# Sixteen-head cross-attention of a gated transformer block: one score pass with exponentials kept by row, or two score passes with transposed exponentials

## The chip, the cores and the metric

The kernel runs on one core of one Trainium2 chip. The metric is the device time of one execution in microseconds (us); several runs are taken and their median is the number compared.

## The reference, cut to what matters

Two layers act on x of 4 batches x 512 tokens x 128 features, with a context of 4 x 77 rows. The second layer's attention is what the change touches; 16 heads of 8 features attend to the 77 context rows of the batch:

```python
Q = split(LN(x) @ W_q.T); K = split(ctx @ W_k.T); V = split(ctx @ W_v.T)   # 16 heads, 8 wide
scores = einsum('bhqd,bhkd->bhqk', Q, K) / sqrt(8)
scores = where(mask, -inf, scores)          # mask (1, 1, 512, 77)
w = nan_to_num(softmax(scores, -1), nan=0)
x = x + tanh(g_xattn[1]) * (merge(einsum('bhqk,bhkd->bhqd', w, V)) @ W_o.T)
x = x + tanh(g_ffn[1]) * moe(LN(x))          # router (24 columns per token), best 2 of 8 experts, silu(a)*g
```

Ahead of it stand a first layer's single-head attention and a quantised feed-forward layer; behind it 39 expert tiles of 128 rows.

## The kernel before, in words

The program is one hand-ordered list per engine: TensorE (`pe`), VectorE (`dve`), ScalarE (`act`), GpSimd (`pool`) and SyncE (`sp`, loads and stores), tied by semaphores. An engine takes its list strictly in order, so a wait holds back all that stands behind it. PSUM has eight banks of 512 f32: `bank[0]` to `bank[3]` and the four of `wide`.

**Keys and values.** The 16 heads are four groups of four. Group g has its 32 features on partitions 32g to 32g+31 (`qT`, `kblk`), and its 4 x 77 = 308 score columns. `kblk` holds the keys block-diagonally within a group; `vblk` does so for the values, cut into `NCH` = 12 chunks of 103 or 102 score columns (three to a group).

**Attention of a batch, before.** `scores(b, u)` on TensorE (L649, L652) makes a unit of 128 queries x two groups: two bf16 matmuls lay the mask into two banks of `wide`, and two f32 matmuls, each on 32 rows of the array, add the scores. A batch has `UNITS` = 8 units in two buffers. `softmax(b, u)` on VectorE takes the head maxima (L1015) and writes score minus maximum to `pC` in SBUF (L1018); `expC` on ScalarE (L450) makes the exponentials in place; `sums` (L1024) adds them by head, and `sums_end` takes the reciprocals. Then `turn_p(b, c)` on TensorE (L673) turns each of the 12 chunks in four transposes into `bank[2]` or `bank[3]`, `copy_pT` on ScalarE (L458) copies it to SBUF, and `pv(b, t)` (L688) multiplies four chunks at once, in four strips of 32 output rows, into `bank[1]`. The reciprocals are turned and spread over the features by `turn_r`, `copy_rT`, `spread_r`, `copy_rE`; `attn_out` (L1040) multiplies. `wo` (L717) projects, `residual` (L1044) adds to x and takes the statistics and the reciprocal root of the next norm on VectorE.

**Router of a batch.** Step 0 normalises (L867), transposes (L725) and copies; step 1 multiplies by the router weights (L730) and picks experts in a chain of small VectorE operations (L1057 to L1087); step 2 ranks them (L738, L739) and makes the slots (L1091 to L1106). Then `send(b)` on GpSimd writes the batch's rows out with 8 indirect DMAs (L370). `router(b, 0)` waits, from batch 2 on, for the rows of batch b-2.

**Order.** A period n = 0..11 of batch b issues `turn_p(b, n)`, then, for the first eight, unit n of batch b+1, then `pv`. The wo, residual and router steps of batch b-1 stand at fixed slots of the period of batch b (`WO_SLOT`, `NORM_SLOT`, `ROUTER_SLOTS`). Ahead of the first period, the four queries are made (L537, L663) while GpSimd supplies the reciprocal roots (`rsqrt`, L349 to L355) and VectorE finishes the feed-forward layer. Behind the last period stand `wo(3)`, `residual(3)`, the three router steps of batch 3 and `send(3)`; only when all rows have landed do the expert tiles start.

## Time and profile before

| what | us |
|---|---|
| median of 3 runs | 430.97 |
| the three runs | 431.97, 430.97, 419.12 |
| the profiled execution | 425.74 |
| its span, from the first instruction to the last | 424.0 |
| TensorE busy in it | 284.7 |
| VectorE busy in it | 260.5 |
| ScalarE busy in it | 124.3 |
| GpSimd busy in it | 94.5 |
| mean granted TensorE clock, share of full speed | 0.727 |

All rows come from the profiled execution. Its own time is 1.7 us more than its span, and the median of the runs is 5.2 us more than its time. PE is TensorE's matmul, PEld its weight load, DVE VectorE, ACT ScalarE, POOL GpSimd, SP SyncE. A f32 matmul shows as two records (two passes), a bf16 matmul and a transpose as one.

### The profile page before, as it was taken

What the parts mean: (1) busy time and instruction counts of PE and PEld (TensorE: products, weight loads), DVE (VectorE), ACT (ScalarE), POOL (GpSimd) and SP (SyncE); (2) the same over time, 40 slices, a digit from 0 to 9 for tenths busy, and PEclk for the clock granted to TensorE, in tenths of its full rate; (3) what the DMA queues carried; (4) which work ended last, traced back from release to release, by engine and by line L of the source; (5) the groups of instructions that cost most, each with busy time, mean ns of one, the idle gap of its engine ahead of it and who ended that gap; (6) DMA issues with size and microseconds to landing.
All of it is one profiled execution on the core that took longest, in us unless ns stands there. A gap on an engine that the chain in (4) does not pass through costs nothing.

```text
span 424.0 us, 5379 instructions
## 1 busy us (share of the span) xinstructions
PE 284.7 (67%) x1571; PEld 197.0 (46%) x1572; DVE 260.5 (61%) x754; ACT 124.3 (29%) x240; POOL 94.5 (22%) x157
## 2 busy tenths in 40 slices
PE   1158824634689798989798875732039998999920
PEld 0158712113233343545355434412038998989920
DVE  5746995987737887597769854755403433444424
ACT  1022105435215354423343243301023333333300
POOL 8300000003710000000250033060602444434420
PEclk9999965556555598755675567565559999999975
DMA  7993001500000000000010000010356767768337
GB/s 225 364 336 115 2 5 8 138 1 0 1 2 0 0 2 0 2 0 0 12 41 0 0 22 32 0 51 0 100 175 195 210 204 199 210 198 226 109 97 206
DMA packets 34787, 36.96 MB, mean 87 GB/s; under 512 B 8990, under 2 KB 26901, under 8 KB 34767
## 3 DMA queue, kind: packets, MB, share of 16 engines
q1 hardware_dynamic: 30607, 23.73, 20.7%
q0 software_dynamic: 4160, 12.99, 8.7%
q8 instruction: 9, 0.15, 0.1%
q14 instruction: 11, 0.09, 0.1%
HBM read 22.52 MB, written 14.49 MB: 87 GB/s over the span
## 4 chain that ended last, share of the span: by engine, by line
PE 43%; DVE 35%; issue 8%; DMA 5%; POOL 4%; ACT 3%; SPq 1%; POOLq 0%; DVEq 0%; ACTq 0%
PE wide L786 13%; PE bank L795 6%; PE bank L673 4%; PE wide L652 4%; DVE space L1018 3%; DVE mC L1015 3%; PE bank L688 3%; DVE st L838 2%; DVE amh L989 2%; DVE h L867 2%; DVE space L985 2%; DVE sC L1024 2%; DMA space<-expert_out 2%; PE bank L717 2%; POOL expert_rows L370 2%
## 5 line engine op out<-in xcount | busy, mean ns | idle before, releaser
L370 POOL DMA_INDIRECT expert_rows<-pay,slot x32 | 30.8, 963 | 158.9 <-DVE slot L1106 150.4
L1156 DVE TENSOR_TENSOR space<-space,wide 128x384 f32<-128x384 f32 x39 | 21.6, 554 | 66.0 <-PE wide L786 55.2
L786 PE MATMUL wide<-space,w1r 128*128 128x128 f32 x468 | 60.8, 281 | 0.0
L786 PEld LDWEIGHTS wide<-space,w1r 128*128 128x128 f32 x468 | 57.0, 197 | 0.4
L379 POOL DMA_INDIRECT expert_out<-space x39 | 38.3, 982 | 60.9 <-DVE space L1163 60.6
L673 PE MATMUL bank<-ident,space 128*103 128x128 f32 (+1 forms) x192 | 42.0, 368 | 13.2 <-ACT pTC L458 7.1
L673 PEld LDWEIGHTS bank<-ident,space 128*103 128x103 f32 (+1 forms) x192 | 32.0, 211 | 33.5 <-issue 16.3
L450 ACT ACTIVATE space<-space 128x616 f32<-128x616 f32 x32 | 22.8, 716 | 58.5 <-DVE space L1018 58.3
L652 PE MATMUL wide<-kblk,h2T 32*128 32x308 f32 x128 | 38.1, 686 | 0.0
L1015 DVE TENSOR_REDUCE mC<-wide 128x8 f32<-128x616 f32 x32 | 25.4, 795 | 19.3 <-PE wide L652 16.4
L458 ACT ACTIVATE pTC<-bank 103x512 f32<-103x512 f32 (+1 forms) x48 | 27.8, 587 | 23.6 <-PE bank L673 16.2
L795 PE MATMUL bank<-w_s,space 128*128 x234 | 32.6, 275 | 0.2 <-DVE space L1156 0.2
L537 PE MATMUL bank<-ident,h 128*128 128x128 f32 x48 | 13.3, 433 | 28.6 <-DVE h L867 27.8
L795 PEld LDWEIGHTS bank<-w_s,space 128*128 128x128 f32 x234 | 29.3, 192 | 0.3 <-issue 0.3
L505 ACT ACTIVATE space<-bank 128x128 f32<-128x128 f32 x39 | 10.8, 277 | 60.7 <-PE bank L771 58.3
L1018 DVE TENSOR_TENSOR space<-wide,mC 128x616 f32<-128x616 f32 x32 | 25.6, 799 | 1.1
L771 PE MATMUL bank<-ident,space 128*128 128x128 f32 x39 | 11.4, 293 | 21.7 <-DMA space<-expert_rows 17.2
L537 PEld LDWEIGHTS bank<-ident,h 128*128 128x128 f32 x48 | 8.6, 217 | 35.8 <-DVE h L867 34.9
L511 ACT ACTIVATE space<-wide 128x384 f32<-128x384 f32 x39 | 19.1, 490 | 17.0 <-PE wide L786 16.2
L1024 DVE TENSOR_REDUCE sC<-space 128x16 f32<-128x1232 f32 x16 | 22.5, 1425 | 0.0
L649 PE MATMUL wide<-mneg,identb 128*128 128x308 bf16 x64 | 19.8, 404 | 1.5 <-DVE space L1018 1.5
L349 POOL TENSOR_SCALAR rvp<-mv 128x4 f32<-128x4 f32 x4 | 0.9, 224 | 87.0 <-DVE mv L841 86.6
(205 smaller groups left out, 432.9 us busy)
## 6 DMA issues: line engine op xcount, KB each, us to landing
w1r<-in_w1T SPq DMA_DIRECT2D x39, 352.0 KB
expert_rows<-blank POOLq DMA_DIRECT2D x2, 2970.0 KB, 18.3
expert_rows<-blank POOLq DMA_DIRECT2D x1, 2574.0 KB, 28.3
space<-expert_rows SPq DMA_DIRECT2D x39, 66.0 KB
space<-expert_out SPq DMA_DIRECT2D x8, 256.0 KB, 3.2
xs<-in_x SPq DMA_DIRECT2D x4, 256.0 KB, 3.8
w_s<-in_w2T SPq DMA_DIRECT2D x2, 512.0 KB, 5.1
out<-xs SPq DMA_DIRECT2D x4, 256.0 KB, 3.4
```

The source lines that it names most:

```text
L370: pool.indirect_dma_start(tbl, bass.IndirectOffsetOnAxis(ap=slot[:, k, t:t + 1], axis=0), pay[:, b % 2, k, j, :], None).then_inc(rows_sent ...
L379: pool.indirect_dma_start(planes, bass.IndirectOffsetOnAxis(ap=mpay[:, j, D:D + 1].bitcast(I32), axis=0), my[:, j, :], None, bounds_check= ...
L450: act.activation(p, p, ACT.Exp, scale=float(DH) ** -0.5).then_inc(pC_ready, 1)
L458: act.activation(pTC[0:w, q % (2 * NG), :], bank[2 + q % 2][0:w, :], ACT.Copy).then_inc(pTC_ready, 1)
L537: ins = pe.transpose(bank[0][:, j * P:(j + 1) * P], src[:, j, :], ident[:])
L652: ins = pe.matmul(o[i], qT[r, b, j * P:(j + 1) * P], kblk[r, :, b * KS:(b + 1) * KS], start=False, stop=True)
L673: ins = pe.transpose(bank[2 + q % 2][0:w, j * P:(j + 1) * P], pC[:, (b * TB + j) % (2 * TB), c0:c0 + w], ident[:])
L786: ins = pe.matmul(wide[:, 2 * p + g, c * P:(c + 1) * P], w1r[:, q, g * F + F0[c]:g * F + F0[c] + P], mhT[:, p, :])
L795: ins = pe.matmul(bank[1 + p][:, 0:D], mhidT[:, p, c, :], w2_s[:, bass.ds(w + c * D, D)], start=(c == 0), stop=(c == NF - 1))
L1015: link(dve.tensor_reduce(m.rearrange("p (g l) -> p g l", g=2), s, AX.X, ALU.max))
L1018: dve.tensor_tensor(pC[:, t % (2 * TB), (u % 2) * HU:(u % 2 + 1) * HU].rearrange("p (g l k) -> p g l k", g=2, l=HG), s, m.rearrange("p (g ...
L1024: dve.tensor_reduce(sC[:, j, :], pC[:, (b * TB + j) % (2 * TB), :].rearrange("p (h k) -> p h k", h=H), AX.X, ALU.add).then_inc(sums_done, 1)
```

## The change

**Two score passes.** The first pass only finds maxima: `quad_max(b, j)` makes the scores of 128 queries and all four groups, four mask matmuls and then four f32 matmuls on the four 32-row strips of the array, and `max_of` takes the maxima in two reductions. `split_max` clips them at FLOOR, negates them and splits them into three bf16 parts that stand in `comb` beside the mask; `turn_max` transposes `comb` (bf16), `copy_comb` copies it. The second pass, `quad_exp(b, t)`, makes the scores transposed, keys on partitions and 512 queries in the free dimension: four bf16 matmuls of `pick` with `combT` lay down minus maximum and mask, four f32 strip matmuls add the scores. `expT` takes the exponential straight from PSUM to `pT`, four of 103 (or 102) x 512. There are no transposes of p, no subtraction, no `expC` over SBUF and no copies of p.

**Sums.** `pv` works in two halves of 256 queries; beside the four matmuls with `vblk` it has four with `hones`, which leave each head's sum beside the output in the same bank. `recip` on ScalarE takes Ln (with a bias TINY) and Exp(-x), and `attn_out` on VectorE corrects it by one step, three operations of 128 x 256 for each half. `turn_r`, `spread_r` and their copies go.

**Banks.** The quads take two pairs of banks each from a ring of three pairs (`wide` and the new `duo`). Quad n waits until the second pair of quad n-2 and the first pair of quad n-1 are read.

**Order.** The four quads of maxima of batch 0 are made among the queries. A period of batch b is: exp 0, pv half 0 of b-1, max 0 and 1 of b+1, pv half 1 of b-1, rank of b-2, exp 1, max 2, wo of b-1, max 3, exp 2, turn_max(b+1), router steps 0 and 1 of b-1. So a router begins at the end of a period and ends in the next one; behind the last period stand the second half of router 2's step 1, its step 2, and all of router 3. `misc` keeps the users of `bank[0]` apart. The next norm's reciprocal roots of batches 0 and 1 move from VectorE to GpSimd, ahead of `send(0)` in its list. GpSimd also makes `hones` and `pick`, by memsets and six affine selects, and copies the mask. One activation table with both Ln and Exp is loaded by hand ahead of the first exponential.

```diff
-    UNITS = 2 * TB
-    RT_SLOT, WO_SLOT, NORM_SLOT, ROUTER_SLOTS = 0, 2, 4, (5, 6, 9)
+    NPART = 3
+    KM = NPART * H
+    KROWS = KM + KS
+    HS = S // 2
+    TR = NCH // NG
...
+        quads = [("max", 0, j) for j in range(TB)]
+        for b in range(NB):
+            for t in range(TR):
+                quads.append(("exp", b, t))
+                if b + 1 < NB and t < 2:
+                    quads += [("max", b + 1, 2 * t), ("max", b + 1, 2 * t + 1)]
+        pairs = [wide[:, 0:2, :], wide[:, 2:4, :], duo[:]]
...
-            for n in range(2 * NB, 3 * NB):
+            for n in range(2 * NB, 3 * NB + 2):
                 rsqrt(n)
...
+            def expT(b, t, pair_no):
+                if pair_no == 0:
+                    act.wait_ge(sT_psum, TR * b + t + 1)
...
+                for i in range(2):
+                    c = NG * t + 2 * pair_no + i
+                    w = HCH[c][1]
+                    act.activation(pT[0:w, (NCH * b + c) % (2 * NCH), :], pair("exp", b, t, pair_no)[0:w, i, :], ACT.Exp,
+                                   scale=float(DH) ** -0.5).then_inc(pT_ready, 1)
+            def recip(b, half):
...
+                act.activation(lnS[:, n % 2, :], obank(b, half)[:, HS:S], ACT.Ln, bias=tiny[:]).then_inc(ln_ready, 1)
+                act.wait_ge(ln_ready, n + 1)
+                act.activation(rE[:, n % 2, :], lnS[:, n % 2, :], ACT.Exp, scale=-1.0).then_inc(rE_ready, 1)
...
+            def pairs_free(n):
+                for place in (2 * n - 3, 2 * n - 2):
+                    if place >= 0:
+                        pe.wait_ge(*emptied(place))
+            def quad_max(b, j):
...
+                for g in range(NG):
+                    pe.matmul(o[g].rearrange("p (l k) -> p l k", l=HG), identb[:],
+                              mneg[:, j, None, :].broadcast_to([P, HG, KS]), start=True, stop=False)
+                for g in range(NG):
+                    r = slice(32 * g, 32 * g + 32)
+                    ins = pe.matmul(o[g], qT[r, b, j * P:(j + 1) * P], kblk[r, b, :], start=False, stop=True)
+                ins.then_inc(sC_psum, 1)
...
+            def quad_exp(b, t):
...
+                for g in range(NG):
+                    pe.matmul(o[g], pick[0:KROWS].rearrange("p h k -> p (h k)")[:, g * GC:(g + 1) * GC][:, keys(t)],
+                              combT[0:KROWS, b % 2, :], start=True, stop=False)
+                for g in range(NG):
+                    r = slice(32 * g, 32 * g + 32)
+                    ins = pe.matmul(o[g], kblk[r, b, keys(t)], qT[r, b, :], start=False, stop=True)
+                ins.then_inc(sT_psum, 1)
...
                 for g in range(NG):
-                    pe.matmul(bank[1][32 * g:32 * g + 32, :], vblk[0:w, c, b, :], pTC[0:w, (q + g) % (2 * NG), :],
-                              start=(t == 0), stop=(t == 2)).then_inc(pv_done, 1)
+                    pe.matmul(o[32 * g:32 * g + 32, 0:HS], vblk[0:w, NG * t + g, b, :], pT[0:w, (q + g) % (2 * NCH), cols],
+                              start=(t == 0), stop=False)
+                for g in range(NG):
+                    ins = pe.matmul(o[32 * g:32 * g + 32, HS:S], hones[0:w, t, :], pT[0:w, (q + g) % (2 * NCH), cols],
+                                    start=False, stop=(t == TR - 1))
...
+            for b in range(NB - 1):
+                quad_exp(b, 0)
+                if b >= 1:
+                    for t in range(TR):
+                        pv(b - 1, 0, t)
+                quad_max(b + 1, 0)
+                quad_max(b + 1, 1)
+                if b >= 1:
+                    for t in range(TR):
+                        pv(b - 1, 1, t)
+                if b >= 2:
+                    router(b - 2, 2)
+                quad_exp(b, 1)
+                quad_max(b + 1, 2)
+                if b >= 1:
+                    wo(b - 1)
+                quad_max(b + 1, 3)
+                quad_exp(b, 2)
+                turn_max(b + 1)
+                if b >= 1:
+                    router(b - 1, 0)
+                    router(b - 1, 1)
...
+            def max_of(b, j):
+                dve.wait_ge(sC_psum, TB * b + j + 1)
+                for i in range(2):
+                    dve.tensor_reduce(mC[:, b % 2, j, i * 2 * HG:(i + 1) * 2 * HG].rearrange("p (g l) -> p g l", g=2),
+                                      pair("max", b, j, i)[:, :, 0:GC].rearrange("p g (l k) -> p g l k", l=HG),
+                                      AX.X, ALU.max).then_inc(max_ready, 1)
...
+            def split_max(b):
...
+                link(dve.tensor_scalar(c[:, :, 0:H], m, FLOOR, -1.0, ALU.max, ALU.mult))
+                link(dve.scalar_tensor_tensor(out=mR[:], in0=m, scalar=FLOOR, in1=c[:, :, 0:H], op0=ALU.max, op1=ALU.add))
+                link(dve.tensor_scalar(c[:, :, H:2 * H], mR[:], -1.0, None, ALU.mult))
+                dve.scalar_tensor_tensor(out=c[:, :, 2 * H:KM], in0=mR[:], scalar=-1.0, in1=c[:, :, H:2 * H],
+                                         op0=ALU.mult, op1=ALU.subtract).then_inc(split_ready, 1)
+            def attn_out(b, half):
...
+                link(dve.tensor_tensor(z, o[:, HS:S], r, ALU.mult))
+                link(dve.scalar_tensor_tensor(out=z, in0=z, scalar=-2.0, in1=r, op0=ALU.add, op1=ALU.mult))
+                dve.scalar_tensor_tensor(out=oT[:, half * HS:(half + 1) * HS], in0=o[:, 0:HS], scalar=-1.0, in1=z,
+                                         op0=ALU.mult, op1=ALU.mult).then_inc(oT_ready, 1)
...
+            b = NB - 1
+            router(b - 2, 1, 0)
+            attn_out(b - 1, 0)
+            router(b - 2, 1, 1)
+            attn_out(b - 1, 1)
+            router(b - 2, 2)
+            residual(b - 1)
+            router(b - 1, 0)
+            router(b - 1, 1, 0)
+            attn_out(b, 0)
+            attn_out(b, 1)
+            residual(b)
+            router(b - 1, 1, 1)
+            router(b, 0)
+            router(b - 1, 2)
+            for step in range(1, 3):
+                router(b, step)
```

## Rows read from the trace of the kernel before

**Rows 1.** The page: granted clock in tenths, 40 slices of 10.6 us.
```profile
PEclk9999965556555598755675567565559999999975
```

**Rows 2.** Groups by form: busy us, mean ns | idle us before, releaser.
```profile
L370 POOL DMA_INDIRECT expert_rows<-pay,slot x32 | 30.8, 963 | 158.9 <-DVE slot L1106 150.4 <-issue 8.5
...
L673 PE MATMUL bank<-ident,space 128*103 128x128 f32 x128 | 27.5, 353 | 6.0 <-issue 3.2 <-ACT space L450 2.7
L1018 DVE TENSOR_TENSOR space<-wide,mC 128x616 f32<-128x616 f32 x32 | 25.6, 799 | 1.1
L1015 DVE TENSOR_REDUCE mC<-wide 128x8 f32<-128x616 f32 x32 | 25.4, 795 | 19.3 <-PE wide L652 16.4 <-issue 2.8
...
L1024 DVE TENSOR_REDUCE sC<-space 128x16 f32<-128x1232 f32 x16 | 22.5, 1425 | 0.0
...
L458 ACT ACTIVATE pTC<-bank 103x512 f32<-103x512 f32 x32 | 18.6, 585 | 16.8 <-PE bank L673 9.4 <-remote 4.1 <-PE bank L688 3.3
...
L479 ACT ACTIVATE qk<-qk 128x256 f32<-128x256 f32 x4 | 1.7, 416 | 8.1 <-DVE qk L1062 8.1
...
L349 POOL TENSOR_SCALAR rvp<-mv 128x4 f32<-128x4 f32 x4 | 0.9, 224 | 87.0 <-DVE mv L841 86.6 <-POOL rstd L355 0.3
```

**Rows 3.** Windows: us, busy (x records) of PE, PEld, DVE, ACT, POOL; PEclk; DMA.
```profile
119.00:142.00 23.00, 19.27 (x55) 6.48 (x53) 16.25 (x23) 8.35 (x12) 0.00 (x0) 0.50 0.00 0
...
184.00:204.70 20.70, 16.28 (x64) 9.07 (x62) 18.31 (x50) 7.47 (x14) 0.00 (x0) 0.50 0.00 0
204.70:225.00 20.30, 19.29 (x88) 10.49 (x88) 13.54 (x44) 6.99 (x13) 7.86 (x8) 0.67 0.08 27
312.60:405.00 92.40, 86.41 (x736) 84.67 (x737) 34.87 (x77) 31.20 (x79) 36.35 (x37) 0.97 0.66 188
```

**Rows 4.** Timeline of PE, attention: start us, us, line, operands, records, idle.
```profile
125.21 2.07 PE L663 MATMUL bank<-hT,wqT_s 128*128 128x512 f32 x2 [0.69 <-ACT hT L391]
...
131.01 0.69 PE L649 MATMUL wide<-mneg,identb 128*128 128x308 bf16 x2
131.63 1.40 PE L652 MATMUL wide<-kblk,h2T 32*128 32x308 f32 x4
132.96 0.69 PE L649 MATMUL wide<-mneg,identb 128*128 128x308 bf16 x2
...
142.40 1.18 PE L673 MATMUL bank<-ident,space 128*103 128x128 f32 x4 [2.73 <-ACT space L450]
...
160.16 1.07 PE L688 MATMUL bank<-pTC,vblk 103*32 103x512 f32 x8
...
169.06 0.68 PE L673 MATMUL bank<-ident,space 128*103 128x128 f32 x4
...
171.54 0.43 PE L649 MATMUL wide<-mneg,identb 128*128 128x308 bf16 x2
171.90 0.79 PE L652 MATMUL wide<-kblk,h2T 32*128 32x308 f32 x4
...
206.58 3.31 PE L688 MATMUL bank<-pTC,vblk 103*32 103x512 f32 x16
209.82 0.68 PE L673 MATMUL bank<-ident,space 128*103 128x128 f32 x4
...
238.54 1.94 PE L688 MATMUL bank<-pTC,vblk 103*32 103x512 f32 x8
...
250.75 0.68 PE L673 MATMUL bank<-ident,space 128*103 128x128 f32 x4
```

**Rows 5.** Timeline of DVE: router 2, then behind the last pv of batch 3.
```profile
267.84 0.42 DVE L1065 TENSOR_REDUCE qks<-qk 128x32 f32<-128x256 f32 x1 [0.48 <-ACT qk L479]
...
272.51 0.17 DVE L1087 CAST ohs<-qkm 128x32 bf16<-128x32 f32 x1
...
278.23 0.69 DVE L1040 TENSOR_TENSOR oT<-bank,rE 128x512 f32<-128x512 f32 x1 [3.70 <-PE bank L688]
...
298.13 0.17 DVE L1106 CAST slot<-slotf 128x8 int32<-128x8 f32 x1
```

More of the change, by code:

```diff
@@ L210, in flamingo_kernel, with pair, emptied, obank @@
         tbl_v = tbl.rearrange("(p n r) c -> p n (r c)", p=P, r=3)
+        quads = [("max", 0, j) for j in range(TB)]
[4 more added lines that the diff above has]
+                    quads += [("max", b + 1, 2 * t), ("max", b + 1, 2 * t + 1)]
+        quad_no = {q: n for n, q in enumerate(quads)}
+        pairs = [wide[:, 0:2, :], wide[:, 2:4, :], duo[:]]
+        def pair(kind, b, k, i):
+            return pairs[(2 * quad_no[kind, b, k] + i) % 3]
+        def emptied(place):
+            kind, b, k = quads[place // 2]
+            if kind == "max":
+                return max_ready, 2 * (TB * b + k) + place % 2 + 1
+            return pT_ready, NG * (TR * b + k) + 2 * (place % 2 + 1)
+        def obank(b, half):
+            return bank[2] if b == NB - 1 and half else bank[1][:]
+        def keys(t):
+            return slice(THIRD * t, THIRD * t + HCH[NG * t][1])
         def xb(b):
@@ L318, in _ @@
                                     pattern=[[1, P]], channel_multiplier=-1))
-            for t, p_, c_, n_ in ((headof, 1, -DH, H), (spread, -DH, 1, P)):
+            for t, p_, c_, n_ in ((headof, 1, -DH, H),):
                 link(pool.memset(t[:], 1.0))
@@ L677, in pv @@
-            def pv(b, t):
+            def pairs_free(n):
[3 more added lines that the diff above has]
+            def quad_max(b, j):
+                n = quad_no["max", b, j]
+                if n == 0:
+                    pe.wait_ge(mneg_ready, 1)
+                if n == 1:
+                    pe.wait_ge(dn_ready, NB)
+                if j == 0:
+                    pe.wait_ge(q_ready, b + 1)
+                pairs_free(n)
+                o = [pair("max", b, j, g // 2)[:, g % 2, 0:GC] for g in range(NG)]
+                for g in range(NG):
[5 more added lines that the diff above has]
+                ins.then_inc(sC_psum, 1)
@@ new lines, in turn_max @@
+            def turn_max(b):
+                misc(combT_ready, b + 1)
+                pe.wait_ge(split_ready, b + 1)
+                if b == 0:
+                    pe.wait_ge(mneg_copied, 2)
+                for j in range(TB):
+                    ins = pe.transpose(bank[0][:].bitcast(BF16)[0:KROWS, j * P:(j + 1) * P], comb[:, b % 2, j, :], identb[:])
+                ins.then_inc(comb_psum, 1)
+            def quad_exp(b, t):
+                if b == 0 and t == 0:
+                    pe.wait_ge(pick_made, 1)
+                if t == 0:
+                    pe.wait_ge(combT_ready, b + 1)
+                pairs_free(quad_no["exp", b, t])
+                w = HCH[NG * t][1]
+                o = [pair("exp", b, t, g // 2)[0:w, g % 2, :] for g in range(NG)]
+                for g in range(NG):
[5 more added lines that the diff above has]
+                ins.then_inc(sT_psum, 1)
@@ new lines, in _ @@
+            b = NB - 1
+            quad_exp(b, 0)
+            for t in range(TR):
+                pv(b - 1, 0, t)
+            quad_exp(b, 1)
+            for t in range(TR):
+                pv(b - 1, 1, t)
+            router(b - 2, 2)
+            quad_exp(b, 2)
+            wo(b - 1)
+            for t in range(TR - 1):
+                for half in range(2):
+                    pv(b, half, t)
+            router(b - 1, 0)
+            router(b - 1, 1)
+            for half in range(2):
+                pv(b, half, TR - 1)
@@ L1047, in residual, with router @@
                 stats(3 * NB + b)
-            def router(b, step):
+            def router(b, step, half=None):
                 pb = pay[:, b % 2]
@@ L1054, in router @@
                     normalise(3 * NB + b, pb[:, 0, :, 0:D])
-                if step == 1:
+                if step == 1 and half != 1:
                     dve.wait_ge(mix_psum, b + 1)
@@ L1063, in router @@
                                       ALU.subtract).then_inc(qkm_ready, 1)
+                if step == 1 and half != 0:
                     dve.wait_ge(qke_ready, b + 1)
```

330 lines of the change are left out of this document (147 added, 183 removed).

## The prediction

> **What bounds the kernel now.** I read four views in turn. The page's clock slices show TensorE's clock at full speed over the expert tiles and near half over most of the attention, slices 12 to 29 [rows 1]. The windows then show why attention is the place to look: a period of a middle batch takes 40.8 and 40.9 us, from the first transposes at 169.06 to those at 209.82 and 250.75 [rows 4], and two windows that make up such a period (184.0 to 225.0) have TensorE busy 35.6 us (16.28 + 19.29) and VectorE 31.9 us (18.31 + 13.54) at clocks of 0.50 and 0.67, against 0.97 over the expert tiles [rows 3]. So TensorE is nearly full, but at half speed, and VectorE is close behind. The groups say what VectorE does there: maxima, subtractions and sums are 25.4, 25.6 and 22.5 us, and TensorE has 192 transposes of p, 128 of them 27.5 us [rows 2]. The timeline prices the pieces at both speeds. ScalarE and GpSimd have room. The change acts from the first query to the last send; what lies before and behind stays.
>
> **TensorE, work by work.** I give each price at the low clock and, after a slash, at the high one.
>
> A pair of mask matmuls takes 0.62 / 0.36 us (131.01 to 131.63; 171.54 to 171.90), a pair of f32 score matmuls on two strips 1.33 / 0.72 (131.63 to 132.96; 0.79 less the 0.07 by which 1.40 exceeds 1.33) [rows 4]. The trace has no four-strip matmul. Below, it costs what the pair does, since the two of the pair run side by side (four records, 1.40 us); above, twice that. I take the lower end, because pv runs four strips side by side already: 8 records of 512 columns in 1.94 us at the low clock, 1.07 at the high [rows 4]. A quad of maxima is then 2 x 0.62 + 1.33 = 2.6 / 1.4, where the two units it replaces take 3.9 / 2.2. A quad of exponentials has 512 columns for 308: four pick matmuls 1.9 / 1.1, four strips 2.1 / 1.1 (both scaled by columns, less what a pair loses at its ends), together 4.0 / 2.2.
>
> What a page would change in this stands here alone: the Trainium skill, TensorE: Matmul & The Clock Gate, section Measured speedup vs the span model, has four K=32 row tiles of 512 columns gain 3.07 times and not four. By it and the query's matmul (two records in 2.07 us, about 1.87 between starts), a strip set is 4 / 3.07 x 1.87 = 2.4 us and not 2.1, and the sum is about 3 us higher. No row here shows four.
>
> pv of a batch has 3 x 4 matmuls of 512 columns now, about 1.74 / 0.87 a set (the times above less 0.2 of lag); afterwards twice the columns, so 10.4 / 5.2 instead of 5.2 / 2.6. The four bf16 transposes of maxima are an estimate of 0.6 / 0.4. Gone are 12 x 4 transposes of p, about 0.98 / 0.48 each set (1.18 and 0.68 less 0.2) [rows 4], and an estimated 2 us of turned and spread reciprocals. Per middle batch: 4 x 2.6 + 3 x 4.0 + 10.4 + 0.6 = 33.4 against 8 x 1.95 + 11.8 + 5.2 + 2 = 34.6 low; 17.8 against 18.5 high. With wo and router, an estimate of 5.2 / 2.6 on both sides, it is 38.6 / 20.4. **TensorE's work is not cut.** The time can come only from its waits and its clock.
>
> **VectorE and ScalarE.** VectorE loses eight subtractions of 0.80, four sums of 1.43 [rows 2], 0.8 of reciprocals and attn_out's 0.69 [rows 5]: 13.6 us of 31.9. It gains split_max (four small operations, 0.9) and attn_out in six operations of 256 columns at 0.42 plus links (0.42 from L1065 [rows 5]), 2.8: about 22 us. ScalarE has twelve exponentials of 512 columns in place of twelve copies (0.585 each [rows 2]) and eight exponentials; recip is four of 256 columns (at most 0.42 each, L479). It stays under 15 us a batch. One table load stands where one stood.
>
> **The ring.** A quad needs the first pair of the quad just before it read: 0.795 for a reduction, about 1.1 for two exponentials, unless other work lies between. That is a new wait at TensorE, and everything in its list is queued behind it. In batch 0's period nothing lies between: seven waits, 7 us. In a middle period pv or wo cover about half: 4 us. VectorE serves in order too, so a quad of maxima can also wait for router or attn_out chains; 1 to 2 us.
>
> **The clock.** From 119 to 142 us TensorE is busy 19.3 of 23 us, mostly on two-strip scores, at 0.50; the expert tiles, full array, get 0.97 [rows 3]. In the middle batches it was low up to a pv of 16 records at 206.58, and the transposes at 209.82 take 0.68 against 1.18 at 142.40 [rows 4]. [...] The new quads use all four strips, the mask and pick matmuls all rows, pv doubles. I take the high clock for half of each middle period. Both ends (none, all) are rivals below.
>
> **The sum**, against the profiled execution's 425.7 us:
> - Start. The quads of batch 0 fill the waits between queries, TensorE's work is 4 x 2.6 instead of 8 x 1.95, and VectorE's last subtractions, sums and exponentials no longer stand ahead of the first transposes at 142.40. In place come two reductions, split_max, transposes and a copy (about 3.5 us). Bounds 131 and 138; I take 135: -7.4.
> - Period of batch 0, low clock: 3 x 4.0 + 4 x 2.6 + 7 = 29.3 for 26.7 (142.40 to 169.06): +2.6.
> - Two middle periods. Half the time at each clock, 38.6 / 20.4 takes 1 / (0.5/38.6 + 0.5/20.4) = 26.7; with 5.3 of waits 32.0 for 40.85: -17.7.
> - Period of batch 3, 27.5 now (250.75 to 278.23). No maxima of a next batch, but pv of two batches: 3 x 4.0 + 20.8 + 5.2 = 38 / 19.6, at half and half 26, waits 4: +2.5.
> - Tail, 20.1 now (278.23 to 298.30) [rows 5]. attn_out is 2.1 longer. Because routers begin at a period's end, the second half of router 2's step 1 now stands there as well: L1065 at 267.84 to L1087 at 272.68, 4.8 us. Waits for bank 0 and router 2's last step beside router 3's matmuls, 1.4. +8.3.
> - send(2), eight DMAs of 0.96 + 0.30 = 10.1 us [rows 2], starts some 11 us before slot 3 is ready, so it is just hidden; without that, 10.1 us more at most.
> - GpSimd's constants stand in front of an idle time of 86.6 us [rows 2]: nothing. Its two extra reciprocal roots make the next norm later by an estimated 2 us each, at a period's end, inside the waits above; send(0) queues behind them and has a period of slack.
>
> Sum -7.4 + 2.6 - 17.7 + 2.5 + 8.3 = -11.7, so 414.0 us. The runs shown have a median 5.2 above the profiled time and a lowest 6.6 below; I leave the sum where it is and keep that spread for the range.
>
> **Rivals.**
>
> *A, the clock goes up and stays.* For: the argument above, doubled; against: ring waits open gaps. Then the start gives -9, batch 0's period 3 x 2.2 + 4 x 1.4 + 7 = 19.2 (-7.5), the middle ones are bound by VectorE's 22 us and the order of its list, about 30 (-21.7), batch 3 28 (+0.5), tail +8.3: -29.4, 396 us. [...]
>
> *B, slower: the clock stays low through attention.* Place: the three later periods. Middle ones 38.6 + 3 = 41.6 (+0.8 each), batch 3's 38 with the waits mostly hidden against 27.5 (+9.5 to 10.5), start -6, batch 0 +2.6, tail +8.3: about +16, 442 us. It decides from a high share of about a quarter downwards. For: 119 to 142 us at 0.50 with TensorE 84% busy; against: the pv that raised it.
>
> *C, the strips run two by two.* A set costs twice: 16 x 1.0 + 12 x 1.6 at mean clock, 35 us, of which some 5 hide in ring waits: 414 + 30 = 444 us. Against: pv.
>
> *D, waits eat the gain.* If the ring and VectorE's order cost 6 us more in each middle period, it is 426 us. A rule of the skill leans this way: TensorEngine Tiling (Array Packing), Key Properties, says a change of tiling mode drains TensorE; each quad has two. In the trace that drain is inside the 0.62 and 1.33.
>
> **How the numbers follow.** Forecast 0.38, A 0.24, B 0.14, C 0.06, D 0.18. A measurement of this kernel can tell about 2% from no change. The forecast is 2.7% faster and falls within 2% in one case of six; D lies within, with small parts to either side. Faster 0.57, same 0.21, slower 0.22. The range reaches to A and to B: 395 to 440 us; the forecast's own is 405 to 422.
>
> **What would show it.** Right: in a middle period about 32 us with TensorE's clock near 0.75; four-strip sets (eight records) near 1.4 us at the low clock for 308 columns; VectorE busy about 22 us a period and no subtraction group; seven waits near 1 us before quads in batch 0's period; 28 us from the last batch's first attn_out to slot 3. Wrong: four-strip sets of 2.7 us (C), a clock of 0.50 throughout (B) or 1.0 throughout (A), GpSimd still in send(2) when slot 3 is ready.

## The result, and the profile after

The changed kernel takes 419.69 us (median of 20 runs, 417.02 to 421.40), the kernel before 427.77 us (median of 20, 418.65 to 431.97). The ratio is 0.9928, 95% interval 0.9901 to 0.9955: 0.7% faster, no difference at 2%. It is not the quotient of the two medians (0.981), because it leaves out slow runs, those well above the fastest of the same kernel, and only the kernel before had any: it compares with some 422.7 us (419.69 / 0.9928). The forecast was 414.0 us, 2.7% less than the profiled 425.7. The profiled execution took 420.08 us, span 418.3 (before 425.74 and 424.0).

The page's slices, in tenths. The first line is TensorE's row before, the others are the changed kernel's; the clock row answers to [rows 1]. TensorE is busy less in the middle of the span (260.0 us in all, 284.7 before) and clocked higher (0.781 on average, 0.727 before):

```profile
PE   1158824634689798989798875732039998999920
```

```profile
PE   0158725655486668867877974411059899989910
PEclk9999975556568568896887997555559999999975
```

Windows of the changed kernel, one for each step of the forecast: batch 0's period, the two middle ones, batch 3's, and the tail from batch 3's first attn_out to the start of the last send. Columns as in [rows 3]:

```profile
133.50:162.20 28.70, 20.73 (x88) 7.03 (x89) 6.87 (x12) 5.74 (x12) 0.00 (x0) 0.60 0.00 1
162.20:192.70 30.50, 22.63 (x204) 11.35 (x205) 12.26 (x31) 10.47 (x21) 2.77 (x14) 0.91 0.00 1
192.70:227.40 34.70, 26.76 (x208) 13.15 (x208) 19.70 (x75) 9.95 (x21) 5.90 (x17) 0.80 0.01 5
227.40:263.40 36.00, 27.41 (x251) 12.97 (x251) 16.50 (x79) 10.66 (x23) 12.67 (x14) 0.83 0.08 27
263.40:292.80 29.40, 6.01 (x33) 4.58 (x25) 21.26 (x117) 2.83 (x7) 7.67 (x9) 0.50 0.06 19
```

| step | forecast | measured | missed by |
|---|---|---|---|
| first exp quad | 135 us | 133.5 us | -1.5 |
| period of batch 0 | 29.3 | 28.7 | -0.6 |
| two middle periods | 64.0 | 65.2 | +1.2 |
| period of batch 3 | 30.0 | 36.0 | **+6.0** |
| tail | 28.4 | 29.4 | +1.0 |

Four of five steps lie within 1.5 us. Batch 3's period holds nearly the whole error (6.0 us; the four others add up to 0.1). TensorE's timeline in that period shows it: pv sets of eight records come every 0.43 us, and from 249.28 us on, matmuls come one or two at a time, behind gaps for which the profile has no releaser ("issue"):

```profile
248.41 0.61 PE L796 MATMUL bank<-space,hones 103*32 103x256 f32 x8
248.85 0.61 PE L793 MATMUL duo<-space,vblk 103*32 103x256 f32 x8
249.28 0.76 PE L796 MATMUL duo<-space,hones 103*32 103x256 f32 x2
250.36 0.59 PE L796 MATMUL duo<-space,hones 103*32 103x256 f32 x2 [0.32 <-issue]
251.11 0.38 PE L796 MATMUL duo<-space,hones 103*32 103x256 f32 x1 [0.16 <-issue]
251.83 0.42 PE L796 MATMUL duo<-space,hones 103*32 103x256 f32 x2 [0.34 <-issue]
253.25 0.38 PE L796 MATMUL duo<-space,hones 103*32 103x256 f32 x1 [1.00 <-issue]
253.55 0.68 PE L813 MATMUL bank<-ident,pay 128*128 128x128 f32 x2
254.68 0.43 PE L813 MATMUL bank<-ident,pay 128*128 128x128 f32 x2 [0.45 <-issue]
258.49 1.87 PE L819 MATMUL bank<-wqkv_s,hT 128*128 128x24 f32 x8 [3.38 <-ACT hT L443]
```

The chain of waits goes through it as a piece without a name, 10.46 us ahead of ScalarE's copy of router 2's hT:

```profile
245.21 2.06 ACT space L513 x4
247.26 10.46 another core or an unknown queue
257.75 0.60 ACT hT L443
```

The last two transposes are recorded at 254.68, but the copy that waits for them starts 3 us later; ends of matmuls are modelled, so the true ends, or their signals, came later than the rows say. GpSimd's rows say what ran beside it. send(1), eight DMAs, stood from 246.15 to 256.0 us:

```profile
246.15 0.96 POOL L422 DMA_INDIRECT expert_rows<-pay,slot  x1 [12.25 <-DVE slot L1224]
...
255.02 0.96 POOL L422 DMA_INDIRECT expert_rows<-pay,slot  x1 [0.30 <-issue]
```

The trace of before has the same sign beside its own send(1), and it stood in the rows of the forecast: "issue 3.2" at L673 and "remote 4.1" at L458 [rows 2]. Nothing was made of it.

### The profile page after: what moved, and what is told of

Its sections match the earlier page's. It is cut to its first block, busy times and chain, and to the rows that moved or that the text cites. A ratio compares the mean times of both kernels' runs of the same rounds, so it can differ in the third digit from the quotient of the medians.

```text
span 418.3 us, 5818 instructions
## 1 busy us (share of the span) xinstructions
PE 260.0 (62%) x1803; PEld 177.2 (42%) x1804; DVE 219.4 (52%) x710; ACT 105.9 (25%) x220; POOL 107.9 (26%) x193
## 4 chain that ended last, share of the span: by engine, by line
PE 45%; DVE 29%; issue 8%; ACT 5%; POOL 5%; DMA 5%; another core or an unknown queue 3%; SPq 1%; POOLq 0%; DVEq 0%
PE wide L901 13%; POOL expert_rows L422 3%; PE duo L910 3%; PE bank L910 3%; DVE h L982 3%; DVE st L953 2%; DVE mC L1116 2%; ACT space L513 2%; PE wide L750 2%; PE wide L772 2%; DVE amh L1103 2%; DMA space<-expert_out 2%; DVE space L1099 2%; PE bank L793 2%
## 5 line engine op out<-in xcount | busy, mean ns | idle before, releaser
L1116 DVE TENSOR_REDUCE mC<-wide 128x8 f32<-128x616 f32 x22 | 16.9, 791 | 26.2 <-PE duo L750 17.5
L513 ACT ACTIVATE space<-wide 103x512 f32<-103x512 f32 (+1 forms) x32 | 17.0, 601 | 29.0 <-PE wide L776 18.4
L982 DVE TENSOR_SCALAR h<-xs,mv,rstd 128x128 f32<-128x128 f32 x48 | 17.1, 421 | 4.3 <-POOL rstd L391 4.1
L776 PE MATMUL wide<-h2T,kblk 32*103 32x512 f32 (+1 forms) x64 | 17.7, 802 | 0.0
L910 PE MATMUL bank<-w_s,space 128*128 x120 | 16.8, 276 | 0.2 <-DVE space L1287 0.2
L953 DVE BATCH_NORM_STATS2 st<-xs 128x6 f32<-128x128 f32 x64 | 13.8, 279 | 5.2 <-DMA xs<-in_x 4.8
L750 PE MATMUL wide<-kblk,h2T 32*128 32x308 f32 x88 | 16.5, 606 | 0.0
L746 PE MATMUL wide<-mneg,identb 128*128 128x308 bf16 x44 | 11.1, 368 | 8.6 <-DVE mC L1116 3.9
L513 ACT ACTIVATE space<-duo 103x512 f32<-103x512 f32 (+1 forms) x16 | 8.7, 601 | 28.4 <-PE wide L776 28.4
L793 PE MATMUL bank<-space,vblk 103*32 103x256 f32 (+1 forms) x168 | 15.6, 449 | 0.4 <-DVE oT L1156 0.4
## 6 DMA issues: line engine op xcount, KB each, us to landing
space<-expert_out SPq DMA_DIRECT2D x8, 256.0 KB, 3.3
xs<-in_x SPq DMA_DIRECT2D x4, 256.0 KB, 3.7
out<-xs SPq DMA_DIRECT2D x4, 256.0 KB, 3.4
```

The lines of the kernel that those rows point to most:

```text
L513: act.activation(pT[0:w, (NCH * b + c) % (2 * NCH), :], pair("exp", b, t, pair_no)[0:w, i, :], ACT.Exp, scale=float(DH) ** -0.5).then_inc( ...
L750: ins = pe.matmul(o[g], qT[r, b, j * P:(j + 1) * P], kblk[r, b, :], start=False, stop=True)
L793: pe.matmul(o[32 * g:32 * g + 32, 0:HS], vblk[0:w, NG * t + g, b, :], pT[0:w, (q + g) % (2 * NCH), cols], start=(t == 0), stop=False)
L910: ins = pe.matmul(bank[1 + p][:, 0:D], mhidT[:, p, c, :], w2_s[:, bass.ds(w + c * D, D)], start=(c == 0), stop=(c == NF - 1))
L953: ins = dve.bn_stats(st[:, n % 2, j, :], xs[:, (n % NB) * TB + j, :])
L982: ins = dve.tensor_scalar(dst[:, j, :], xs[:, (n % NB) * TB + j, :], mv[:, n, j, 0:1], rstd[:, n, j:j + 1], ALU.subtract, ALU.mult)
```

## The experiments

Kernels of one series ran one after the other on one chip, with the kernel before beside them. The first series is e1 to e4; the changed kernel itself was in none until e12, so up to there its 419.69 us is a number of another series. (The expectations say "call" for a series.)

**1. Is it the instruction fetch?** The trace lists 16 KB packets of TensorE's instruction queue at 232.3 and 247.5 us, each inside a send. 128 increments at the start of TensorE's list move them; 256 put them back.

```diff
+            for _ in range(128):
+                pe.sem_inc(pad, 1)
             pe.wait_ge(ident_made, 1)
             pe.wait_ge(ld_ctx, 48)
             pe.matmul(wide[:, 0, 0:NB * KS], wbT_s[:], ctxT_s[:]).then_inc(mA_psum, 1)
+            for _ in range(128):
+                pe.sem_inc(pad, 1)
```

e1 has the first loop, e2 both.

> The changed kernel with 128 semaphore increments (on a semaphore that nobody waits for) put ahead of TensorE's first wait, where TensorE stands idle until 9.5 us; all else is the same. They move TensorE's program on by 128 instructions, and with it the places at which the instruction queue (q8 in the list of DMA packets) fetches the next 16 KB: from 232.3 and 247.5 us, both beside a send, to about 218 and 240 us, beside none. Theory F (TensorE starves when a fetch falls beside a send of GpSimd): the stall of 249.3 to 257.7 us is gone, batch 3's period takes about 30 us for 36.0, and the time is 412 to 415 us for 419.7. Theory S (a send holds up TensorE or its semaphores whatever TensorE fetches): the stall stays, 419 to 421 us.

> The control of e1_pad128: 256 such increments, 128 ahead of the first matmul and 128 behind it, so that the fetches fall where they fell in the changed kernel. Theory F: the stall is back, 419 to 421 us. If added instructions at the start had an effect of their own (a different clock, a later first matmul), this run would differ from 419.7 us too; then e1_pad128 says less.

e1 422.39 us (10 runs), e2 439.00. The increments take 0.15 us each and were not free: TensorE's first matmul comes at 20.5 us for 9.6, the first exp quad at 135.5 and 153.1 us for 133.5. From there to the end all three take the same, 285.0, 284.2 and 284.8 us. In e1 the packets came at 228.7, 241.3 and 261.4 us, none in send(1) (248.2 to 258.0), and ScalarE still waited:

```profile
ACT hT L444 <- remote: 10.4, 1, 10.4
```

Theory F falls. (The unchanged kernel in e12, below, says it once more: packets at 232.0 and 247.3 us, beside the sends, and no stall.) The Trainium skill (Runtime: NRT & Kernel Launch, Instruction fetch mechanics) has instructions refilled in blocks of 16 KiB, at a cost mostly hidden; that agrees with these packets and with their place making no difference. A fault of the pair: e2 was meant as a costless control and cost 19 us.

**2. Is it the send?** One wait more on GpSimd:

```diff
             for b in range(NB):
+                if b == 1:
+                    pool.wait_ge(mix_read, 3)
                 send(b)
```

> The changed kernel with one more wait on GpSimd: send(1) also waits until router 2's mix is copied (about 255 us if the stall goes), so that nothing is sent beside TensorE's fetch at 247.5 us. Theory F and theory S both take the stall away: 412 to 416 us. Theory B (the boundary of 16 KB alone stalls TensorE, whatever GpSimd does) and theory W (a wait of the new order, not the chip, holds TensorE back): the stall stays, 419 us or more.

414.49 us (4 runs, 413.06 to 415.51). send(1) ran from 253.6 to 263.6 us, and the same stretch of TensorE is whole:

```profile
246.98 0.61 PE L798 MATMUL duo<-space,hones 103*32 103x256 f32 x8
249.59 0.73 PE L815 MATMUL bank<-ident,pay 128*128 128x128 f32 x4 [2.00 <-DVE pay L984]
251.10 1.87 PE L821 MATMUL bank<-wqkv_s,hT 128*128 128x24 f32 x8 [0.78 <-ACT hT L445]
```

Router 2's mix stands 27.9 us behind the first exp quad of its period, for 33.1. So it is the send beside TensorE's work, not the boundary of the fetch (B) and not a wait of the new order (W). How dense that work must be no run tests: the kernel before pauses beside its send(1) too, with sparser work.

**3. Why does VectorE start late?** In the changed kernel one operation on 128 x 16 values (`rv`) takes 4.29 us and ends when GpSimd's memset of `pay` does; the first eight normalises take 6.0 us for 2.3 while GpSimd makes `pick`. First VectorE, then GpSimd:

```profile
9.59 4.29 DVE L969 TENSOR_SCALAR rv<-mv 128x16 f32<-128x16 f32 x1
...
16.49 6.02 DVE L982 TENSOR_SCALAR h<-xs,mv,rstd 128x128 f32<-128x128 f32 x8
```

```profile
8.77 1.40 POOL L372 MEMSET vblk<- 128x1536 f32 x1
...
12.00 1.85 POOL L379 MEMSET pay<- 128x2112 f32 x1
...
16.18 4.46 POOL L405 TENSOR_SCALAR_AFFINE_SELECT pick<-pick 128x1232 bf16<-128x1232 bf16 x3
```

```diff
+            pool.wait_ge(h_ready, 2)
             pool.memset(vblk[:], 0.0).then_inc(vblk_zero, 1)
```

> The changed kernel with GpSimd's work from the memset of vblk to the last select of pick behind a wait for VectorE's first two normalised batches. Theory P (VectorE's tensor_scalar stands still, or goes slower, while GpSimd writes tensors): VectorE's rv takes 0.2 us for 4.3, the first eight normalises 2.3 us for 6.0, and all behind comes 6 to 8 us earlier: 412 to 414 us. Theory Q (the 4.3 us are VectorE's wait for something of its own, such as a load): rv still takes 4 us or more, 418 to 420 us.

413.86 us (4 runs), with the stall still in it. VectorE's rows, `rv` 25 times shorter and the normalises 2.7 times:

```profile
9.56 0.17 DVE L970 TENSOR_SCALAR rv<-mv 128x16 f32<-128x16 f32 x1
...
12.26 2.26 DVE L983 TENSOR_SCALAR h<-xs,mv,rstd 128x128 f32<-128x128 f32 x8
```

Eight microseconds are won there; 5.6 arrive at the first exp quad (127.8 us): batch 2's normalises still stand 7.3 us ahead of the changed kernel's, the weights' maxima 5.9. Theory P holds. The Trainium skill (SBUF — State Buffer, SBUF: two separate sides) has VectorE, in some of its operations, and GpSimd share a pair of ports under an exclusive lock, where the loser blocks for the whole instruction. The trace agrees that rv is blocked, but for more than one instruction: it began during the memset of `vblk` (8.77 to 10.17 us) and ended only with that of `pay`, the sixth GpSimd operation after it (13.88 us). Other operations are not slowed: the small tensor_tensors from 14.8 us on take 0.17 beside GpSimd's memset of `pick` (14.91 to 16.03), as in e4. That ports are what they share is the skill's account; the runs show the blocking alone.

The price of the constants that the change itself adds, alone:

```diff
+            pool.wait_ge(h_ready, 2)
             link(pool.memset(hones[:], 1.0))
```

> The changed kernel with only the constants that the change adds on GpSimd (the row-sum ones and pick) behind the wait for VectorE's first two normalised batches; the memsets that the kernel before has too stay where they were. If e4's gain of 5.8 us is two parts, this one is the smaller: VectorE's rv still takes 4.1 us (behind the old memsets), the first eight normalises 2.3 us for 6.0, and the attention comes about 2 to 3 us earlier: 416.5 to 418 us for 419.7. If the selects of pick hold VectorE up wherever they stand, the normalises of batches 2 and 3 take it instead and nothing is gained.

413.12 us: far more gained than expected, 6.6 us less than the changed kernel. The attention began 1.5 us earlier (132.0 for 133.5; one profile says little here, as three profiles of the unchanged kernel have 133.5, 133.3 and 131.3), and, unforeseen, the stall was gone. That had to be explained before anything else was read.

**4. A first answer that fell.** In the changed kernel, e1 and e4 TensorE had run some 115 to 120 records, matmuls and weight loads together, from send(1)'s start when it stalled. To see whether their number matters, the middle third of batch 3's keys was left out of pv:

```diff
-            for t in range(TR - 1):
-                for half in range(2):
-                    pv(b, half, t)
+            for half in range(2):
+                pv(b, half, 0)
```

> The changed kernel with the sixteen key-third-1 groups of batch 3's value product left out (both halves, products and sums alike), so that TensorE has some 64 records fewer between the start of send(1) and router 2's transposes; batch 3's attention then lacks those keys. In the four traces with a stall TensorE had run 115 to 119 records from the send's first instruction when it began to trickle. Theory C (what stalls TensorE is the number of its instructions beside a send): with about 80 records ahead of the transposes they run at once behind router 2's normalise (251.9 us), hT is copied by 254 us and router 2's mix by 256 us for 260.5. Theory D (any instruction of TensorE that falls a few microseconds into a send is held until the send ends): the transposes' semaphore comes about 1.7 us behind the send's end again, the mix at 260 us.

415.13 us (one run): no stall, mix at 256.2 us. By its expectation that is theory C. But e9, in a series after it, ran 145 records beside the same send and did not stall either. Both series differed from the first in something that was in no kernel. So the changed kernel itself was run again.

> The changed kernel unchanged, beside e13 on one chip. The stall of TensorE beside the sends was there in the four runs of the first call (e1 to e4, where send(1) stood in its place, and beside send(0) in all four) and in none of the seven runs of the two later calls (e5, e9 and the others, send(0)'s too), e9 with as many TensorE instructions beside its send as the changed kernel. Theory K (the stall belongs to the chip or the occasion, not to the program): this run shows it or not as e13 does, and their times differ by e9's earlier start alone, 1.5 to 2 us. Theory Z (it belongs to the program: where its sends and TensorE's groups meet): this run stalls for some 8 us again, its mix 2 comes 33 us behind the first exp quad of batch 3, and it is 5 to 7 us slower than e13.

> e9_consts_late once more, beside e12. Theory K: stall or none as in e12, and 1.5 to 2 us faster than it. Theory Z: no stall (mix 2 some 28 us behind the first exp quad of batch 3), 411.5 to 413.5 us.

> e4_pool_late once more. Theory K: stall or none as in e12, 5.8 us faster than it. Theory Z: it stalls again (mix 2 35 us behind the first exp quad of batch 3), 413.5 to 415.5 us, slower than e13 though its start is 4 us earlier.

**The changed kernel, unchanged, took 414.50 us** (4 runs, 414.24 to 414.74; ratio 0.9805, 0.968 to 0.993), e13 412.62 and e14 409.81. None of the three profiles has the stall: ScalarE's wait has its name back, and the pv sets run on beside send(1), which stood from 244.5 to 254.2 us. e12's waits and timeline:

```profile
ACT hT L443 <- PE bank L813: 5.9, 1, 5.9
```

```profile
248.69 0.61 PE L793 MATMUL duo<-space,vblk 103*32 103x256 f32 x8
249.12 0.61 PE L796 MATMUL duo<-space,hones 103*32 103x256 f32 x8
251.90 1.08 PE L813 MATMUL bank<-ident,pay 128*128 128x128 f32 x4 [2.17 <-DVE pay L982]
253.75 1.87 PE L819 MATMUL bank<-wqkv_s,hT 128*128 128x24 f32 x8 [0.78 <-ACT hT L443]
```

Theory K holds over Z: the stall goes with the occasion, and within a series all profiled kernels with a send in TensorE's way have it or none. To see whether it comes back:

> The changed kernel a third time, as the yardstick of e16 and e17. Where the stall beside the sends is absent, as in e12: 414 to 415 us; where it is present, as in the first traces: 417 to 421 us.

> e3_send_late once more. If its gain was the stall's alone: beside a stalling e15 4.5 to 6 us faster than it, beside one without a stall no faster, 414 to 415.5 us. If the later send gains for another reason (its descriptors away from other work), it is 3 us or more faster than e15 either way.

> e8_all_three once more beside its yardstick. Gains by e14 (4.7 us of the constants) and by e7's order of the tail (2 us): without a stall 6 to 8 us faster than e15, with a stall 11 to 14 us faster; 405 to 408.5 us either way, since send(1) stands clear of TensorE's dense stretch.

It came back: 419.98 us for the changed kernel (10 runs, 417.54 to 421.62), 414.36 for the later send, 406.30 for the combined kernel. This series ran on the chip of e9 to e11, where nothing had stalled, so it is not the chip alone. All runs of the stall's question, in us:

| kernel | where it stalls | where it does not |
|---|---|---|
| changed kernel | 419.69, 419.98 (e15) | 414.50 (e12) |
| send(1) later | 414.49 (e3), 414.36 (e16) | |
| all GpSimd constants later | 413.86 (e4) | 409.81 (e14) |
| the change's constants later | | 413.12 (e9), 412.62 (e13) |
| all three (e8, below) | 406.30 (e17) | 406.40 (e8) |

A later send(1) takes the stall's price away, 5.2 us (across series) and 5.6 us (e16 against e15, in one), and lands where the unstalled kernel is. e5 says nothing of the stall then; its one run is no faster without a third of batch 3's pv (415.1 for 414.5).

**5. What the four strips are worth.** Each quad written two strips at a time:

```diff
-                for g in range(NG):
-                    pe.matmul(o[g].rearrange(...), identb[:], ...)
-                for g in range(NG):
-                    r = slice(32 * g, 32 * g + 32)
-                    ins = pe.matmul(o[g], qT[r, ...], kblk[r, b, :], start=False, stop=True)
+                for two in (range(0, 2), range(2, 4)):
+                    for g in two:
+                        pe.matmul(o[g].rearrange(...), identb[:], ...)
+                    for g in two:
+                        r = slice(32 * g, 32 * g + 32)
+                        ins = pe.matmul(o[g], qT[r, ...], kblk[r, b, :], start=False, stop=True)
```

(and the same in `quad_exp`)

> The changed kernel with each quad's matmuls written pair by pair (two masks or max rows and two scores, then the other two), so that only two array strips run beside each other; banks, ring and order stay. A set over four strips takes 1.41 us for 308 columns and 2.05 us for 512 at the low clock and 0.80 and 1.12 us at the high one; a set over two took 1.40 us for 308 in the kernel before. A middle period has four of the first and three of the second. Theory T (the gain of the middle periods is the four strips): 6.6 us (high clock) to 11.8 us (low) more in each period, four periods, less what waits hide: 436 to 450 us. Theory V (VectorE and the waits for banks bound the periods, the strips are cover): under 4 us a period, 420 to 432 us.

467.48 us (4 runs, 463.16 to 469.40), 53 more than the unstalled kernel and more than theory T allowed. First a set on four strips, from e12, then on two, from e6, both at the high clock; they take the same:

```profile
167.38 0.80 PE L750 MATMUL wide<-kblk,h2T 32*128 32x308 f32 x8
```

```profile
192.51 0.79 PE L751 MATMUL wide<-kblk,h2T 32*128 32x308 f32 x4
193.23 0.44 PE L747 MATMUL wide<-mneg,identb 128*128 128x308 bf16 x2
193.60 0.79 PE L751 MATMUL wide<-kblk,h2T 32*128 32x308 f32 x4
```

So a quad pays for its strips twice. The rest is the clock. e6's windows of the periods of batches 1 and 2 have it at 0.70 and 0.61, where the changed kernel has 0.91 and 0.80:

```profile
181.40:224.70 43.30, 38.15 (x204) 15.55 (x205) 12.47 (x31) 10.47 (x21) 2.78 (x14) 0.70 0.00 1
224.70:273.10 48.40, 43.26 (x209) 16.89 (x208) 19.87 (x75) 9.96 (x21) 9.92 (x22) 0.61 0.03 9
```

Busy time times clock is 26.7 and 26.4 us there, for 20.6 and 21.4 in the changed kernel: an estimate of 6 and 5 us more work a period at the high clock (theory T said 6.6). The periods grow by 12.8 and 13.7 us, so the lower clock costs the larger half. Why it is lower the rows do not say. On two strips the new order is slower than the kernel before, whose middle periods take 40.9 us.

**6. The tail, and the best kernel.** e7 is e3 with router 3's first round over TensorE opened before router 2 is finished:

```diff
             residual(b)
-            router(b - 1, 1, 1)
             router(b, 0)
+            router(b - 1, 1, 1)
             router(b - 1, 2)
```

(TensorE's and ScalarE's lists: router 3's step 0 ahead of router 2's step 2.) e8 adds e4's wait.

> e3_send_late with router 3's normalise put ahead of the second half of router 2's step 1 on VectorE, and its transposes and copy ahead of router 2's rank on TensorE and ScalarE, so that they run while VectorE works on router 2. Theory R (router 3's round over TensorE stands open behind residual(3), 3.2 us of VectorE idle ahead of mix 3): mix 3 comes 2.5 to 3 us earlier, and the last send 2.1 us earlier, as GpSimd's send(2) then ends last: 412 to 413 us for e3's 414.5. Theory G (GpSimd's sends bound the tail now, nothing is gained): 414 to 415 us.

> e7_tail_order with e4's wait ahead of GpSimd's constants as well. If the three gains add (5.2 us of send(1), 2.1 of the tail, 5.8 of the constants, each at its own place on the path): 406 to 408 us. If the earlier attention meets another low stretch of TensorE's clock, or a send beside dense work of TensorE, part of it is given back: 409 to 413 us.

e7 412.42 us, e8 **406.40 us** (4 runs, 405.16 to 408.73; ratio 0.9562, 0.943 to 0.970) and, as e17, 406.30 (ratio 0.9667, 0.960 to 0.974: the kernel before was faster in that series). From residual(3) to the end of the last send the changed kernel takes 34.1 us, e7 32.4 and e8 32.6: 1.6 us gained. GpSimd is as late as VectorE then: send(2) ends in the moment in which slot 3 is ready (278.0 us in e8). e7's 2.1 us under e3 are from another series, so its share is read from that stretch. Against the changed kernel in its own series e17 is 13.7 us faster.

**7. Two parts undone.** The inverse roots of batch 1's router go back to VectorE (in e8): the three ranges end at `3 * NB + 1` instead of `3 * NB + 2`.

> e8_all_three with the inverse roots of batch 1's router (stats 13) back on VectorE, as before the change, so that GpSimd sends slot 0 when it is ready (207.9 us) and not 8.3 us later. If send(0)'s place costs the microsecond of stall in its last part, and VectorE has room for 2 us in that period: 404.5 to 406 us. If the extra roots on VectorE lie on its path in that period: 407 to 409 us for e8's 406.4.

410.51 us (4 runs), 4.1 more than e8 in another series: against the first theory, and past the second's 409. The roots now stand between residual and the last maxima. VectorE in e11, then in e8:

```profile
213.05 0.38 DVE L961 BATCH_NORM_AGGREGATE mv<-st 128x2 f32<-128x6 f32 x4
...
215.73 0.80 DVE L1121 TENSOR_REDUCE mC<-wide 128x8 f32<-128x616 f32 x1
```

```profile
211.15 0.38 DVE L961 BATCH_NORM_AGGREGATE mv<-st 128x2 f32<-128x6 f32 x4
211.45 0.77 DVE L1121 TENSOR_REDUCE mC<-wide 128x8 f32<-128x616 f32 x1
```

2.4 us more of VectorE ahead of reductions that free a bank go with 4 us more in that period (38.7 for 34.7). The period is tied to VectorE's order, though VectorE is busy 57% of it (19.70 of 34.70 us in the changed kernel).

The kernel before with e3's wait:

> The kernel before with e3's wait: send(1) waits until router 2's mix is copied. Its trace has the same sign beside send(1), 249.1 to 258.9 us: TensorE pauses from 256.2 until 259.0 us. If that pause is the same stall and lies on the path, it goes and the time falls by 2 to 3 us, to a ratio of 0.993 to 0.995; if it is hidden, or send(2), which now stands behind send(1), comes late, the ratio is 0.998 to 1.005. Either way the gain is smaller than e3's 5.2 us, as TensorE's instructions come less densely here.

425.42 us (5 runs), ratio 1.012 (1.001 to 1.024): no gain. The later send(1) ran into send(2), which starts right behind it at 269.4 us. Its series was one without the stall, so what the pause of 3 us in before's trace costs stays open.

## Why the prediction was off, and where it was right

**The forecast's sum came out for the kernel where TensorE runs freely, in part by luck.** e12 took 414.50 us for 414.0. Its windows of batch 3's period and of the tail are 31.6 and 28.7 us, for the forecast's 30.0 and 28.4:

```profile
227.10:258.70 31.60, 26.23 (x251) 12.94 (x251) 16.59 (x79) 10.66 (x23) 12.66 (x14) 0.77 0.10 31
258.70:287.40 28.70, 5.26 (x33) 4.04 (x25) 21.26 (x117) 2.83 (x7) 7.68 (x9) 0.56 0.06 19
```

The luck is in the middle periods, where two errors cancel. The clock was high for more than the half that was assumed: a mean of 0.91 and 0.80 is the high clock for 0.82 and 0.60 of the time. By the forecast's own prices (38.6 / 20.4 and 5.3 of waits) that makes 27.6 and 30.4 us, 58.0 together. They took 65.2, so 7.2 us more went into waits than were put in.

**The step that failed** is the period of batch 3, +2.5 in the sum, measured +8.5. The sends were priced on GpSimd alone, "just hidden" and with "a period of slack"; at TensorE they were put at nothing. Beside TensorE's work they can hold it, for 4.4 us of this period (36.0 for e12's 31.6). All of it comes beside send(1). The end of send(0) holds TensorE too: the first two exp quads of batch 3 stand 8.24 us apart for e12's 6.78. But the third then ran at the high clock (1.04 and 1.12 us for e12's 1.63 and 2.05), and wo began at 245.14 us for e12's 244.91, no later than the period itself (227.38 for 227.10). Batch 3's period without a stall is 1.6 over the forecast. What the change altered there is that pv of batch 3 has twice the matmuls, in sets of 0.43 us, and that send(1) falls on it; that e3 and e16 lose the stall shows that the place of the send matters, and the part of the denser pv is not shown. That the size depends on the occasion could not be read from one trace; that there is such a pause could, from L673's issue and L458's remote wait.

**The base of the ratio** was one profiled execution, 425.7 us. The ratio compares with some 422.7 us, and against that 414.0 would have been 2.1% and not 2.7%; e12, which took the forecast's time, has 0.9805.

**Another step was wrong and did not show.** The constants on GpSimd, put at nothing, cost 1.9 us (e13 against e12). Their place was argued from an idle time of GpSimd, where the question was what VectorE does beside them. The start came out 1.5 us better than forecast all the same.

**The extra roots on GpSimd** were put at a small loss inside waits. They are a gain of 4.1 us for the one that was undone.

**Rivals.** A, the clock, came in part: high for 0.82 and 0.60 of the middle periods, with part of its gain lost in waits as said. What the forecast read of the clock from before's trace does not carry it. From 148.4 to 160.1 us that trace has it at 1.00 over two-strip scores and transposes, ahead of any pv, and from 175.3 to 206.5 us at 0.50 over the same two with wo, the router and pv among them:

```profile
148.40:160.10 11.70, 10.82 (x64) 5.70 (x62) 10.41 (x13) 6.90 (x12) 0.00 (x0) 1.00 0.01 1
175.30:206.50 31.20, 26.78 (x104) 15.99 (x101) 25.85 (x75) 10.70 (x20) 0.00 (x0) 0.50 0.00 1
```

So the half was a guess, and what decides the clock stays open. One of the 20 runs had a mean clock of 0.855 and took 417.7 us, 2 us under the median. B did not come. C did not come: a set of four strips takes 1.41 us at the low clock, the pair's 1.40, as taken from pv. The Trainium skill's factor of 3.07 (TensorE: Matmul & The Clock Gate, Measured speedup vs the span model) would have given 2.4 us for 512 columns; the set takes 2.05 (e12, at 242.93 us), so the measurement decides for the full factor here. D, waits, came in part: the 7.2 us above are 3.6 a middle period where D had 6. In batch 0's period they came near the forecast size, 1.29 us for exponentials and 1.01 for a reduction (1.1 and 0.795 forecast). Timeline of TensorE, changed kernel; the brackets are the waits:

```profile
150.92 0.43 PE L746 MATMUL wide<-mneg,identb 128*128 128x308 bf16 x2 [1.29 <-ACT space L513]
...
153.36 1.19 PE L746 MATMUL wide<-mneg,identb 128*128 128x308 bf16 x4 [1.01 <-DVE mC L1116]
154.48 1.41 PE L750 MATMUL wide<-kblk,h2T 32*128 32x308 f32 x8
```

**The tail** (routers begin at a period's end) cost nearly what was forecast, +9.3 for +8.3, and send(2) was hidden by 2 us. VectorE was busy 12.3 and 19.7 us in the middle periods, less than the 22 forecast for each; over the whole span it lost 41.1 us (260.5 to 219.4), 10.3 a batch for the forecast's 9.9.

**What stays open** is how a send holds TensorE, and what on an occasion turns it on. Shown: it needs a send beside TensorE's matmuls (e3, e16), it is not where the 16 KB fetches fall (e1), the profiled kernels of a series share it, and the same chip had it once and once not. VectorE's chain of 0.2 us links went on beside it. The runs do not say which resource the two share.

## What to carry to other kernels

Price a transfer not only on the engine that issues it: look at what every other engine does while it runs, and where a send has slack, try it at another place. The gap without a releaser in a trace, at an engine and at those that wait for it, is the sign to look for. Before reading an experiment against a kernel that ran on another occasion, run that kernel again beside it; here the missing stall of e5 and e9 looked like an effect of their edits and was not. Bulk memsets on GpSimd belong where VectorE has nothing to do, not where GpSimd has nothing to do.

## What the hardware showed that was not expected

- A program of the same instructions took 414.5 or 419.7 to 420.0 us depending on the occasion, steady within each (0.5 us spread over 4 runs in e12; 4.4 over 20 and 4.1 over 10 where it stalls).
- While it stalls, TensorE passes one to three records of a set at steps of 0.7 to 1.5 us, where four records passed in 0.22 us before. In e4 the steps lasted until some 2 us behind the end of the send's last instruction (250.04 us); the last row's seven records spread over 1.9 us and end them:

```profile
245.85 0.42 PE L794 MATMUL duo<-space,vblk 103*32 103x256 f32 x2 [0.86 <-issue]
247.26 0.65 PE L794 MATMUL duo<-space,vblk 103*32 103x256 f32 x2 [1.00 <-issue]
248.69 0.58 PE L794 MATMUL duo<-space,vblk 103*32 103x256 f32 x1 [0.78 <-issue]
...
250.12 2.51 PE L797 MATMUL duo<-space,hones 103*32 103x256 f32 x7 [0.79 <-issue]
```

- An operation of 0.17 us on VectorE took 4.3 us beside a run of GpSimd's memsets, in the kernel before too (5.1 us).
- Semaphore increments in TensorE's list take about 0.15 us each: e2's second 128 fill the 18.4 us between the end of its first matmul and the start of the next.
